# Attention windows: masks written by the gathering engine, a tile behind each gather, and rows weighed by ScalarE

## What is computed

```python
edge_features = concatenate([h[dst_idx], h[src_idx] * dir_w, dir_w, lower_adj_feat], axis=-1)
edge_attr = edge_features @ W_ee + b_ee
h_cur = h
for i in range(3):
    residual = h_cur @ W_res + b_res if i == 0 else h_cur
    q, k, v, e = projections(h_cur, edge_attr)
    ke = k[src] + e
    alpha = (q[dst] * ke).sum(-1) / sqrt(C)
    ex = exp(alpha - segment_max(alpha, dst)[dst])
    w = ex / (segment_sum(ex, dst)[dst] + 1e-16)
    out = segment_sum((v[src] + e) * w[:, :, None], dst).mean(over heads)
    h_cur = relu(out + h_cur @ Ws + bs + residual)
return concatenate([h, h_cur]) @ W_ctr + b_ctr
```

## Time and profile before

| what | value |
|---|---|
| median of 3 runs | 4367.55 us (4361.53 to 4377.33) |
| profiled execution, its own time | 4329.4 us |
| its span | 4327.6 us |
| mean granted TensorE clock | 0.916 |
| busy: PE, VectorE, ScalarE, POOL | 3495.6, 1823.4, 1433.0, 1862.8 us |
| gathers of the attention layers, line 2293 | 1344, mean 1006 ns, 964.3 us idle before them |

### The profile page before, as it was taken

How to read it: one execution, slowest core, us unless ns; L and a number is a source line. 1 busy time by engine, 2 the same in 40 slices (tenths; PEclk the granted TensorE clock), 3 DMA queues, 4 the chain that set the end, 5 groups by cost and what they waited for, 6 DMA issues and landing times. The chain is left out here.

```text
span 4327.6 us, 82914 instructions
## 1 busy us (share of the span) xinstructions
PE 3495.6 (81%) x22381; PEld 2067.5 (48%) x22381; DVE 1823.4 (42%) x5369; ACT 1433.0 (33%) x3483; POOL 1862.8 (43%) x1907
## 2 busy tenths in 40 slices
PE   4999999947758888876777777667777769999998
PEld 2666666635534444443444444334443444555564
DVE  4666666647523333332333333323333323344222
ACT  3555555522623333332233323222222223122112
POOL 2555555500256665653566656456666630000000
PEclk8999999979879999998888998878898889999999
DMA  5677775656444554555666666556666645443223
GB/s 139 187 200 199 198 196 167 165 115 204 140 136 137 140 136 131 139 137 136 169 176 172 176 175 179 156 155 167 167 164 168 166 111 176 171 177 118 74 97 125
DMA packets 716528, 675.29 MB, mean 156 GB/s; under 512 B 382359, under 2 KB 542945, under 8 KB 716117
## 3 DMA queue, kind: packets, MB, share of 16 engines
q1 hardware_dynamic: 622598, 466.26, 37.1%
q0 software_dynamic: 77008, 200.24, 17.2%
q10 hardware_dynamic: 16768, 6.91, 0.6%
HBM read 530.84 MB, written 142.28 MB: 156 GB/s over the span
## 5 line engine op out<-in xcount | busy, mean ns | idle before, releaser
L2293 POOL DMA_INDIRECT l_y<-s_lrows,l_src x1344 | 1352.6, 1006 | 964.3 <-issue 352.4
L2373 PE MATMUL ps<-l_y,aw_pT 128*63 128x277 f32 x2700 | 436.8, 467 | 259.9 <-ACT aw_pT L2591 249.1
L3404 PE MATMUL ps<-nl_adj,nl_table 126*128 126x504 bf16 (+1 forms) x3150 | 631.4, 357 | 2.3 <-DVE nl_table L3639 2.3
L998 POOL DMA_INDIRECT em_gs<-s_rows,em_idx x400 | 432.3, 1081 | 325.8 <-DVE em_a L1189 147.9
L2357 PE MATMUL ps<-aw_yT,aw_qt 128*63 128x384 f32 x1800 | 377.2, 529 | 120.0 <-DMA aw_yT<-s_dxT 61.2
L3404 PEld LDWEIGHTS ps<-nl_adj,nl_table 126*128 126x128 bf16 x3150 | 301.8, 96 | 299.0 <-issue 5.3
L2750 DVE COPY aw_axd<-ps 128x252 f32<-128x252 f32 x225 | 94.7, 421 | 796.9 <-remote 409.9
L2330 PE MATMUL ps<-ident,l_y 128*128 128x128 f32 x1800 | 281.5, 292 | 150.9 <-issue 83.1
L2373 PEld LDWEIGHTS ps<-l_y,aw_pT 128*63 128x63 f32 x2700 | 195.7, 154 | 431.9 <-ACT aw_pT L2591 279.6
L2591 ACT ACTIVATE aw_pT<-ps 128x381 f32<-128x381 f32 x225 | 109.9, 488 | 736.8 <-remote 506.0
L2577 ACT ACTIVATE aw_yT<-ps 128x512 f32<-128x512 f32 (+1 forms) x525 | 261.4, 536 | 245.2 <-remote 114.7
(11 more groups left out here) (381 smaller groups left out, 5866.1 us busy)
## 6 DMA issues: line engine op xcount, KB each, us to landing
nl_adj<-s_adj SPq DMA_DIRECT2D x20, 3100.8 KB
aw_yT<-s_dxT SPq DMA_DIRECT2D x150, 384.0 KB
aw_geoS<-s_geoS SPq DMA_DIRECT2D x450, 94.5 KB
nl_adj<-s_adj SPq DMA_DIRECT2D x15, 2325.6 KB
ws_msg<-s_msg SPq DMA_DIRECT2D x75, 384.0 KB, 3.8
s_dxT<-aw_yT SPq DMA_DIRECT2D x75, 384.0 KB
aw_qt<-s_qt SPq DMA_DIRECT2D x225, 126.0 KB
s_msg<-em_msg SPq DMA_DIRECT2D x100, 256.0 KB
```

The lines of the kernel that those rows point to most:

```text
L998: pool.indirect_dma_start(out=gs[:, u, j, :], out_offset=None, in_=d["rows0"], in_offset=bass.IndirectOffsetOnAxis(ap=slot[:, u, 2 * j:2 * ...
L2293: pool.indirect_dma_start(out=y[:, u, j, 0:W], out_offset=None, in_=table, in_offset=bass.IndirectOffsetOnAxis(ap=src[:, u, j:j + 1], axis ...
L2373: m = nc.tensor.matmul(k.ps[64 * v:64 * v + HW, SUM, 0:SW], pT[:, SLOT[u], j, 64 * v:64 * v + HW], y[:, u, v * TH + j, 0:SW], start=j == 0 ...
L3404: m = nc.tensor.matmul(k.ps[:, bank(i, p), 0:cols * WN], source[:, p, q, b, :], adj[:, a % 2, 0:cols, b * WN:(b + 1) * WN], start=b == 0 a ...
```

## The change

- POOL's two inner waits (before the third and fifth gather) are gone. Behind each gather of window w it copies one tile's share of the mask of window w - 2: 21 numbers of a half, spread over the three heads, 128x63 bf16 (`tensor_copy` in the new `mask`). Before the first of six it waits for VectorE's comparison of w - 2. The last two windows' masks come after the loop.
- VectorE's `weigh` and its second mask step are gone. `select` compares for window w + 3, with "not equal" (1 where the slot is another node's), after the mask of the window five earlier was copied. `far` is -2^100 in exchange.
- ScalarE's new `weigh` multiplies the initial rows of w + 2, tile by tile, with the weight as its scale: three behind the exponentials, three behind the copy of the sums. At a layer's head it weighs windows 0 and 1 before the sweep; for l = 0 window 0's weighing stands between the first copies of turned rows.
- PE waits for POOL's mask before the `far` products, and for l > 0 for ScalarE's weighing before the sums. Two semaphores of the query preparation are merged into others (left out below, with a code path that doesn't run on this input).

```diff
@@ -218,7 +218,7 @@
             pool.wait_ge(made, 9)
-            for m, fill in ((k.far, FAR), (k.centre, 1.0 - 1.0 / D)):
+            for m, fill in ((k.far, -FAR), (k.centre, 1.0 - 1.0 / D)):
                 pool.affine_select(out=m[:, :], in_=m[:, :] if m is k.centre else zero[:, 0:128], compare_op=ALU.not_equal, fill=fill,
@@ -2165,7 +2165,9 @@
     agr_ok = steps("agr_ok", ["AG"], U, NW)
-    ready = steps("ready", ["DX", "SEL", "OFF"], U, NW)
+    ready = steps("ready", ["DX"], U, NW)
+    selected = steps("selected", ["SEL"], U, NW)
+    masked = steps("masked", ["OFF"], U, NW)
     soft = steps("soft", ["MAX", "NEG", "DEN", "INV"], U, NW)
@@ -2276,6 +2278,14 @@
     def gpsimd(pool):
+        def mask(w, u, j):
+            if j == 0:
+                pool.wait_ge(selected.sem, selected.of(w, "SEL"))
+                pool.sem_inc(hop["pool"], 1)
+            m = nc.gpsimd.tensor_copy(off[:, u, j:j + 1, :, :], bc(sel[:, u, j:j + 1, :].unsqueeze(2), [128, 1, H, HN]))
+            if j == T - 1:
+                m.then_inc(masked.sem, 1)
+
         def gather(w, u):
@@ -2284,24 +2294,24 @@
             for j in range(T):
-                if started(w, U) and j == 2:
-                    pool.wait_ge(scored.sem, scored.of(w - 3, "S"))
-                    pool.sem_inc(hop["pool"], 1)
-                if started(w, U) and j == 4:
-                    pool.wait_ge(turned.sem, turned.of(w - 2, "T1"))
-                    pool.sem_inc(hop["pool"], 1)
                 pool.indirect_dma_start(out=y[:, u, j, 0:W], out_offset=None, in_=table,
...
                                         ).then_inc(rows_in[u], 16)
+                if started(w, 2):
+                    mask(w - 2, (u - 2) % U, j)
 
...
             before.rows_stored(pool)
+        masked.prime(pool)
         for u in range(1 if before is None else 0, U):
...
                 gather(U * i + u, u)
+        for u in (U - 2, U - 1):
+            for j in range(0, T, 1):
+                mask(NW - U + u, u, j)
 
@@ -2341,7 +2351,7 @@
                                  geoS[:, u, v * HS:(v + 1) * HS].rearrange("f (p j) -> f j p", j=TH), start=True, stop=False)
-            pe.wait_ge(ready.sem, ready.of(w, "OFF"))
+            pe.wait_ge(masked.sem, masked.of(w, "OFF"))
             for j in range(TH):
@@ -2368,6 +2378,8 @@
             pe.wait_ge(agr_ok.sem, agr_ok.of(w - 1, "AG"))
+            if l:
+                pe.wait_ge(ready.sem, ready.of(w, "DX"))
             for j in range(TH):
@@ -2577,6 +2589,20 @@
 
+        def weigh(w, u, i, js):
+            if 0 in js:
+                act.wait_ge(rows_in[u], (i + 1) * 16 * T + rows_base[u])
+                act.sem_inc(hop["act"], 1)
+                act.wait_ge(in_[u], (i + 1) * 96 + in_base)
+                act.sem_inc(hop["act"], 1)
+                if started(w, U):
+                    act.wait_ge(summed.sem, summed.of(w - U, "AG"))
+                    act.sem_inc(hop["act"], 1)
+            for j in js:
+                m = nc.scalar.activation(y[:, u, j, D:2 * D], y[:, u, j, W - D:W], ACT.Copy, scale=y[:, u, j, G0:G0 + 1])
+            if T - 1 in js:
+                m.then_inc(ready.sem, 1)
+
         def exponentials(w, u):
@@ -2629,6 +2655,9 @@
             exponentials(w, u)
+            ahead = not (isinstance(w, int) and w + 2 >= NW)
+            if ahead:
+                weigh(w + 2, (u + 2) % U, i if u < U - 2 else i + 1, range(0, T // 2))
             if queries and started(w, U + 3):
@@ -2638,6 +2667,8 @@
                 copy_sums(w - 1, (u - 1) % U)
+            if ahead:
+                weigh(w + 2, (u + 2) % U, i if u < U - 2 else i + 1, range(T // 2, T))
             if not last and l == 0:
@@ -2651,10 +2682,12 @@
             before.vector_done(act)
-        for s in (yT_ok, pT_ok, exped, agr_ok) + ((query_ok,) if queries else ()):
+        for s in (ready, yT_ok, pT_ok, exped, agr_ok) + ((query_ok,) if queries else ()):
             s.prime(act)
         if before is None:
-            for n in TURNS:
+            copy_features(0, 0, 0, 0)
+            weigh(0, 0, 0, range(T))
+            for n in TURNS[1:]:
                 copy_features(0, 0, n, 0)
@@ -2663,8 +2696,10 @@
                 copy_features(0, 0, n, 0)
+            weigh(0, 0, 0, range(T))
         for to, from_ in weights2:
             act.dma_start(to, from_).then_inc(w2_in, 16)
+        weigh(1, 1, 0, range(T))
         sweep(act, turn)
@@ -2707,22 +2742,12 @@
 
-        def weigh(w, u, i):
-            dve.wait_ge(rows_in[u], (i + 1) * 16 * T + rows_base[u])
-            dve.wait_ge(in_[u], (i + 1) * 96 + in_base)
+        def select(w, u):
             if started(w, U):
-                dve.wait_ge(summed.sem, summed.of(w - U, "AG"))
-            nc.vector.tensor_tensor(y[:, u, :, D:2 * D], y[:, u, :, W - D:W], bc(y[:, u, :, G0:G0 + 1], [128, T, D]),
-                                    ALU.mult).then_inc(ready.sem, 1)
-
-        def mask(w, u):
-            s = ready.sem
+                dve.wait_ge(masked.sem, masked.of(w - U, "OFF"))
             nc.vector.tensor_tensor(sel[:, u, :, :], bc(k.iota_wn[:, 0:HN].unsqueeze(1), [128, T, HN]),
                                     bc(k.dl[:, bass.ds(w, 1), :].rearrange("p w t -> p (w t)").unsqueeze(2), [128, T, HN]),
-                                    ALU.is_equal).then_inc(s, 1)
-            dve.wait_ge(s, ready.of(w, "SEL"))
-            nc.vector.tensor_scalar(off[:, u, :, :, :], bc(sel[:, u, :, :].unsqueeze(2), [128, T, H, HN]), -1.0, None,
-                                    ALU.add).then_inc(s, 1)
+                                    ALU.not_equal).then_inc(selected.sem, 1)
 
@@ -2804,9 +2829,8 @@
                 indices(w + U - 1, (u - 1) % U)
-            if not (isinstance(w, int) and w == NW - 1):
-                weigh(w + 1, (u + 1) % U, i if u < U - 1 else i + 1)
-                mask(w + 1, (u + 1) % U)
+            if not (isinstance(w, int) and w + 3 >= NW):
+                select(w + 3, (u + 3) % U)
             if started(w, 1):
@@ -2827,7 +2851,7 @@
             before.scalar_done(dve)
-        for s in (ready, soft, indexed, parts_ok, out_ok) + ((geo_ok,) if queries else (joined_ok,)):
+        for s in (selected, soft, indexed, parts_ok, out_ok) + ((geo_ok,) if queries else (joined_ok,)):
             s.prime(dve)
@@ -2837,8 +2861,8 @@
             dve.sem_inc(indexed.sem, U)
-        weigh(0, 0, 0)
-        mask(0, 0)
+        for u in range(3):
+            select(u, u)
         sweep(dve, turn)
```

More of the change, by code:

```diff
@@ L2140, in attention_windows @@
         xs = sb("xs", [D, CW])
-        w2_in, query_mixed, query_mixed_c = sem("w2_in"), sem("query_mixed"), sem("query_mixed_c")
+        w2_in = sem("w2_in")
         rows_out, qt_out, qs_out, next_src = sem("rows_out"), sem("qt_out"), sem("qs_out"), sem("next_src")
@@ L2467, in mix_queries @@
                                          start=True, stop=True)
-                m.then_inc(query_mixed, 1)
+                m.then_inc(mixed, 1)
             elif n == 1:
-                pe.wait_ge(query_mixed_c, 2)
+                pe.wait_ge(mixed_c, steps + 2)
                 for h in range(2):
                     m = nc.tensor.matmul(k.ps[:, 6 + h, 0:2 * D + GK], wqT[:, h * D:(h + 1) * D], kb[:, h, :], start=True, stop=True)
-                m.then_inc(query_mixed, 1)
+                m.then_inc(mixed, 1)
             else:
-                pe.wait_ge(query_mixed_c, 4)
+                pe.wait_ge(mixed_c, steps + 4)
                 nc.tensor.matmul(k.ps[:, 6, 0:2 * D + GK], wqT[:, 2 * D:3 * D], kb[:, 2, :], start=True, stop=True)
@@ L2513, in turn @@
                 if queries:
-                    pe.wait_ge(query_mixed_c, 7)
+                    pe.wait_ge(mixed_c, steps + 7)
                 pe.wait_ge(mixed_c, steps)
@@ L2770, in mix_queries @@
         def mix_queries(n):
[L2771 removed]
+            dve.wait_ge(mixed, n + 2)
             if n == 0:
[L2773 removed]
+                nc.vector.tensor_copy(wqT[:, :], k.ps[:, 6, 0:H * D]).then_inc(mixed_c, 1)
                 nc.vector.tensor_copy(kb[:, :, D:2 * D + GK], k.ps[:, 7, 0:H * (D + GK)].rearrange("p (h f) -> p h f", h=H)
[L2775 removed]
+                                      ).then_inc(mixed_c, 1)
             elif n == 1:
                 for h in range(2):
[L2778 removed]
+                    nc.vector.tensor_copy(abc[:, h, :], k.ps[:, 6 + h, 0:2 * D + GK]).then_inc(mixed_c, 1)
             else:
[L2780 removed]
+                nc.vector.tensor_copy(abc[:, 2, :], k.ps[:, 6, 0:2 * D + GK]).then_inc(mixed_c, 1)
                 bias_of = k.ps[:, 7, 0:3 * H].rearrange("p (h t) -> p h t", t=3)
[L2782 to L2783 removed]
+                nc.vector.tensor_copy(ab[:, :, 0:2], bias_of[:, :, 0:2]).then_inc(mixed_c, 1)
+                nc.vector.tensor_copy(ab[0:GK, :, 2:3], bias_of[0:GK, :, 2:3]).then_inc(mixed_c, 1)
         def split_geometry(c):
```

9 lines of the change are left out of this document (1 added, 8 removed).

## The result

The changed kernel takes 4526.86 us (median of 4 runs, 4507.19 to 4540.3), the kernel before 4364.54 (4353.01 to 4377.33): a ratio of 1.0368, 95% interval 1.0318 to 1.0417. It is slower by 162 us where I had forecast 4234 and a gain. The profiled execution took 4530.61 us against 4329.4.

The account below looks back on a forecast made before the run. No engine was full; POOL's gathers and a pause from PE's late signals set the 9.92 us turn. A 9.45 us turn gave -99 us and the heads -35, together -134, applied to the median 4367.55: 4234 us, range 4130 to 4650.

Parts of the forecast that it names:

- POOL's masks: Six copies a turn behind POOL's gathers, 0.24 us each; gathers 1.50 us apart, six taking 9.0 us.
- the pause of 2.1 us: POOL's idle time each turn, read as waiting for the gathers' backlog; expected to go at the new cadence.
- The backlog's size: Behind POOL's gathers: 0.16 us a gather, inferred from two streams; worked off at about 1.40 us, issued each 1.25.
- is three turns old when PE needs it: Under waits: PE's added wait for POOL's mask costs nothing, except at heads and tails.
- The masks' own time: POOL's six copies a turn, 0.24 us each, within a turn of 9.45 us against 9.92.
- VectorE and ScalarE: VectorE's lost weighing worth nothing by itself, but gather stretching goes; ScalarE's added weighing, 1.8 us a turn, hidden.
- my 0.34 us: Stretching of POOL's six gathers a turn beside VectorE's weighing, expected to go; 71 us in the sum.
- The heads: Starts of the three layers: POOL resumes gathers 15, 12 and 7.5 us earlier, together 35 us, bounds 0 and 35.
- S1: Rival, 0.15: the hold stays, POOL's inner waits as valves go; 11.0 us a turn, about 4600 us, or over 5000.
- S2: Rival, 0.10: a gather can't be prepared while POOL copies; cadence 1.97, turn 11.8 us, about 4750 us.
- S3: Rival, 0.05: ScalarE's weighing delays the chain through ScalarE by 0.9 us a turn; 4522 us.

Follow-up runs that it names:

- twice_again: The changed kernel with every mask copy on POOL done twice, once into a spare buffer, on chip 9: 4309.75 us, 0.9949 of the kernel before.
- no_valves: The kernel before with only POOL's two inner waits taken out, on chip 11: 3759.56 us, 0.9982 of the kernel before.
- weigh_on_scalar: The changed kernel with POOL's inner waits put back and the masks written by VectorE, weighing on ScalarE, chip 11: 3724.27 us, 0.9893 of the kernel before.
- weigh_on_vector: The changed kernel with POOL's inner waits put back and the weighing back on VectorE, masks on POOL, chip 11: 4236.17 us, 1.126 of the kernel before.
- masks_and_weigh: The changed kernel with the weighing back on VectorE, masks on POOL, no inner waits, chip 9: 4464.59 us, 1.0282 of the kernel before.

## Why the prediction was wrong

- **The step that failed** is the new cadence under "POOL's masks": "0.95 + 0.01 + 0.24 + 0.30 = 1.50 us ... above the 1.40 at which backlog forms, so the pause of 2.1 us goes". The copy was right (0.25), the gap was not: a gather behind a copy follows after 0.16 us, not 0.30, and takes 0.97, so the change issues a gather each 1.385 us. The pause stayed: 2.56 us of idle time in the mean before a turn's first gather. I had taken the gap from the earlier trace rows and bounded it above by the earlier trace rows (0.79), never below.
- **The backlog's size was wrong too.** By its rule 1.385 us leaves 0.015 us of backlog a gather for 0.15, a tenth, so most of the pause should have gone all the same. It didn't: in the long pause above the signals still came 1.4 us behind the last gather. Nor does the lateness end above 1.40: at 1.55 us PE's scores at the head of layer 0 were 3.6 us late. The head of the change fits the rule only roughly (4.4 us behind the stream's end, less 18 x 0.135 = 2.4, gives 2.0; 2.6 measured).
- **The direction stood.** Where signals are held, a thinner stream lets them pass sooner. Over the turns in which VectorE waited for the scores, they were seen 3.1 us late in the median before (1.25 us apart), 1.0 in the change and 0.2 in twice_again, against 0.05 on the first kind. In these traces the scores also fall at different places in the stream, so the spacing is not the only thing that differs. A value of spacing at which the hold ends is not shown.
- **The depth was missed.** "The mask of window w ... is three turns old when PE needs it; ... Nothing" took POOL to be five windows ahead of PE. With POOL as the bound PE stands right behind it, so a mask of w behind the gathers of w + 2 reaches PE a stream later than the rows it needs anyway. On a chip of the first kind this costs 93 us. On the recorded one I put the pauses of 5.5 us down to it as well, since the held signals lie between that mask and the sums POOL waits for; that is read from one such turn, and how the depth and the hold share the loss there was not measured.
- **The masks' own time** was hidden in my sum behind the pause that was to go. Where no signal is held it is plain: the 227 us between 3993 and 3767 are 188 for the six copies and 93 for the depth, less 54 that ScalarE's weighing and the waits give back. So the change loses there without any hold.
- **VectorE and ScalarE** were right in sign: on chip 11 the gathers take 1001 ns with the weighing on VectorE (no_valves) and 953 with it on ScalarE (weigh_on_scalar), and that kernel is 42 us faster than before, where my 0.34 us a turn were 71. The Trainium skill's warning ("Perfetto Trace Analysis", Optimizing Scalar/DVE Operations) that GpSimd and VectorE share a port, so that moving work between them might not help, agrees with the outcome: masks on VectorE beat six copies on POOL by 188 us (chip 6) and one copy by 98 (chip 13). What costs there is POOL's own time, not a shared port. Contention shows in weigh_on_vector, 316 ns for 253 a copy. The Trainium skill ("SBUF — State Buffer", Who interferes with whom) states such a contention for reads, and the trace agrees; that a two-input VectorE instruction leaves the gathers alone, the rule which I had set against my 0.34 us, the 1001 for 953 ns contradict.
- **The heads**' 35 us came to nothing, by the same step: in the change's head of layer 0 the signal was held to the stream's end. In twice_again the three heads took 57.3, 47.5 and 47.7 us for the 62.8, 55.3 and 51.0 of the kernel before in the recorded profile.
- **The rivals.** S1 (0.15) came nearest: a pause stays, 10.8 us a turn for its 11.0, and 4527 us for its 4600. But its cause, the removed inner waits, is not shown: on chip 11 taking them out changed nothing, and no such run met a chip that holds signals, where S1 would act. S2 had it the wrong way round, a copy makes the next gather start sooner. S3 fell with weigh_on_scalar. The range held the time only because it reached as far as S1, so that is luck as far as the mechanism goes; the sign and the likeliest case were wrong.

## What to carry to other kernels

When an engine is the bound, whoever waits for it stands right behind it: an operation moved onto that engine costs its time there, less what it takes out of gaps (188 of 342 us here), and one placed behind the data costs depth (two windows behind cost 93 us, one behind nothing). One large copy behind the stream is cheaper than six small ones inside it (119.0 for 341.9 us of copies). Where a forecast hangs on a threshold, bound the term that decides it on both sides, and ask whether the behaviour is the kernel's or the chip's.

## What the runs showed of the hardware

- Six chips ran the kernel before in 3758 to 3773 us, two measurements (the recorded one and chip 9, which may be one chip) in 4365 and 4333, 15 to 16% more. On these two PE's semaphore signals come late behind POOL's indirect DMAs, on the others within 0.20 us. What makes the difference is open. The granted clock is lower as well in the change (0.898 for 0.934) but not with the copies doubled (0.920 and 0.916); what it adds was not measured.
- Where signals are held, a wider spacing of the gathers goes with less lateness. The first scores of layer 0 were seen 22.4 us late at 1.25 us (4.4 behind the stream's end), 15.8 at 1.385 (2.6 behind its end), 9.1 at 1.38 in masks_and_weigh and 3.6 at 1.55, the last two within the stream.
- On POOL a gather starts 0.16 us behind a copy but 0.30 behind a gather, and a second copy 0.18 us behind the start of the first though each is shown with 0.24.
- ScalarE's activation of 128x128 float32 with a scale from SBUF took 399 ns for one, and 0.98 us for three in a row.
